# TensorE's order of tile sums and products, and VectorE's order of comparisons, in the relational layers of a seven-layer graph network

## The reference, cut to what matters

```python
m = c[:, 0:1] * (hs @ bases[0])              # hs = h[src], c = coef[etype]
for b in range(1, bases.shape[0]):
    m = m + c[:, b:b + 1] * (hs @ bases[b])
agg = jax.ops.segment_sum(m, dst, num_segments=h.shape[0])
return agg + h @ loopw + bias                # then relu and a residual, three times
...
xt = jnp.einsum('nd,rde->rne', x, W)         # the second relational network, two layers
agg = jax.ops.segment_sum(xt[rel, src], dst, num_segments=x.shape[0])
return jax.nn.relu(agg + x @ SW + b)
```

## Time and profile before

| | |
|---|---|
| median of 3 runs | 7921.8 us (7919.49 to 7972.01) |
| the profiled execution | 7969.38 us, its span 7967.5 us |
| busy: PE, DVE, ACT, POOL | 67%, 42%, 10%, 73% of the span |
| mean granted PE clock | 0.681 of full |

### The profile page before, as it was taken

The page is one execution under the profiler, slowest core; times in us unless marked ns, Lnnn a source line. Parts: engine busy times, 40 slices in busy tenths (PEclk is TensorE's granted clock), DMA queues, the critical chain, the costliest instruction groups (busy, mean ns, idle before and its releaser), DMA issues. The chain is left out here.

```text
span 7967.5 us, 103222 instructions
## 1 busy us (share of the span) xinstructions
PE 5324.7 (67%) x25966; PEld 4686.8 (59%) x25967; DVE 3378.4 (42%) x9384; ACT 821.6 (10%) x1790; POOL 5813.4 (73%) x6265
## 2 busy tenths in 40 slices
PE   6777777777776666677677776666666676644444
PEld 5666656666655555566666675565655566533333
DVE  5444554444455565644444672222222322312222
ACT  1111111111111111100000001111111111100000
POOL 6777767777767777677777427777767777677776
PEclk8777777777766777655555787777777777755555
DMA  3222222222211211222222552222222222212222
GB/s 108 75 74 74 75 69 72 75 74 75 74 49 51 52 52 52 54 63 63 63 63 62 152 173 52 55 56 55 55 53 53 55 55 55 55 52 56 55 55 54
DMA packets 324367, 531.03 MB, mean 67 GB/s; under 512 B 116072, under 2 KB 179733, under 8 KB 323925
## 3 DMA queue, kind: packets, MB, share of 16 engines
q0 software_dynamic: 186496, 383.17, 17.9%
q1 hardware_dynamic: 89185, 119.37, 5.3%
q10 hardware_dynamic: 48500, 26.51, 1.1%
HBM read 448.44 MB, written 80.14 MB: 66 GB/s over the span
## 5 line engine op out<-in xcount | busy, mean ns | idle before, releaser
L608 POOL DMA_INDIRECT ring<-h_table,edges_i x3328 | 3267.7, 982 | 1095.1 <-issue 1078.2
L877 PE MATMUL sum<-onehot,ring 128*128 128x128 f32 x8320 | 1763.1, 343 | 1120.4 <-DMA ring<-h_table,edges_i 901.5
L877 PEld LDWEIGHTS sum<-onehot,ring 128*128 128x128 f32 x8320 | 1373.9, 233 | 1465.5 <-DMA ring<-h_table,edges_i 1015.8
L1176 DVE TENSOR_TENSOR acc<-msg,acc 128x16 f32 x4160 | 728.0, 175 | 2747.3 <-PE msg L884 2214.9
L884 PE MATMUL msg<-work,mix_w 128*128 128x128 f32 x4992 | 1087.2, 406 | 273.5 <-ACT work L687 270.0
L884 PEld LDWEIGHTS msg<-work,mix_w 128*128 128x128 f32 x4992 | 1010.5, 309 | 348.6 <-issue 341.9
L559 POOL DMA_INDIRECT sorted_rows<-ring,pos_i x832 | 850.8, 1023 | 281.5 <-issue 249.3
L687 ACT ACTIVATE work<-sum 128x512 f32<-128x512 f32 x1040 | 621.3, 597 | 3890.4 <-PE sum L877 3823.5
L608 POOL DMA_INDIRECT ring<-in_x_dram,edges_i x832 | 821.1, 987 | 274.5 <-issue 266.5
L591 POOL DMA_INDIRECT ring<-h_table,pos_i x832 | 794.7, 955 | 274.8 <-issue 274.8
L884 PE MATMUL msg<-work,rel_w 128*128 128x128 f32 x3328 | 739.8, 412 | 183.9 <-ACT work L687 183.0
(11 more groups left out here) (198 smaller groups left out, 3483.7 us busy)
## 6 DMA issues: line engine op xcount, KB each, us to landing
ring<-sorted_rows SPq DMA_DIRECT2D x208, 260.0 KB, 3.0
ring<-h_table,edges_i POOLq DMA_INDIRECT x3328, 2.5
edges_i<-bucket_flat SPq DMA_DIRECT2D x208, 208.0 KB
h_table<-rows ACTq DMA_DIRECT2D x78, 256.0 KB
ring<-in_x_dram,edges_i POOLq DMA_INDIRECT x832, 2.5
ring<-h_table SPq DMA_DIRECT2D x832, 8.0 KB
sorted_rows<-ring,pos_i POOLq DMA_INDIRECT x832, 2.3
ring<-h_table,pos_i POOLq DMA_INDIRECT x832, 2.5
```

The lines of the kernel that those rows point to most:

```text
L608: nc.gpsimd.indirect_dma_start(out=rows_in[:, s, :], out_offset=None, in_=rows_of[:, :], in_offset=bass.IndirectOffsetOnAxis(ap=srcT_i[:, ...
L877: last = nc.tensor.matmul(SUM[q % 2][:, t * KEYS:(t + 1) * KEYS], rows_in[:, 4 * q + t, :], onehot[:, 4 * q + t, :], start=True, stop=True)
L1176: nc.vector.tensor_tensor(acc[:, at], MSG[h][:, s * WIN:(s + 1) * WIN], acc[:, at], ALU.add).then_inc(added, 1)
```

## The change

On PE the function `messages` is taken apart into `tile_sums(h, i, k)` (the sums of a half) and `mix(h, k)` (its products). Before, a turn was sums 0, products 0, sums 1, products 1. Now the sums of half 0 of a layer's first turn stand in `opened`, ahead of the loop, and a turn is sums 1, products 0, sums 0 of the next turn (not in the last turn, by a condition on PE), products 1. On DVE both halves' comparisons of the next turn stand between the additions of half 0 and of half 1; before, those of half 1 were made at the front of their own turn, ahead of `rank` or `settle`. In the layers without a norm the number of chunks written out ahead of the loop goes from 4 to 2.

```diff
+SHORT_LAG = 2
...
-    for c in range(LAG):
+    for c in range(lag):
         step(c, c % 2, c // 2, rounds(c))
-    with eng.Fori(LAG // 2, CHUNKS // 2) as n:
+    with eng.Fori(lag // 2, CHUNKS // 2) as n:
...
                     def opened(p):
                         pe.wait_ge(pass_opened, P * r + p + 1)
                         apart(pe)
+                        tile_sums(0, 0, pe.snap(count(P, p, r, 0)))
...
+                    def tile_sums(h, i, k):
+                        for q in (2 * h, 2 * h + 1):
+                            pe.wait_ge(onehot_ready[q], k + 1)
+                            pe.wait_ge(evacuated[(q + 2) % 4], k + 1)
+                            for t in range(4):
+                                pe.wait_ge(gathered[4 * q + t], i * 16 + (GATHER_PASS * r + 16))
+                                last = nc.tensor.matmul(SUM[q % 2][:, t * KEYS:(t + 1) * KEYS], rows_in[:, 4 * q + t, :],
+                                                        onehot[:, 4 * q + t, :], start=True, stop=True)
+                            last.then_inc(summed[q], 1)
+
+                    def mix(h, k):
+                        for q in (2 * h, 2 * h + 1):
+                            pe.wait_ge(evacuated[q], k + 1 + h)
+                        pe.wait_ge(added, k * RING + HALF * h + HALF)
+                        for n in range(N_RELS):
+                            last = nc.tensor.matmul(MSG[h][:, 0:HALF * WIN], W[:, n, :],
+                                                    sums[:, h, n, :, :].rearrange("p t v -> p (t v)"),
+                                                    start=(n == 0), stop=(n == N_RELS - 1))
+                        last.then_inc(messaged[h], 1)
+
                     def messages(i, k):
...
+                        tile_sums(1, i, k)
+                        mix(0, k)
+                        with pe.If(i < TURNS - 1):
+                            tile_sums(0, nc.s_assert_within(i + 1, min_val=1, max_val=TURNS - 1,
+                                                            skip_runtime_bounds_check_because="the condition above"),
+                                      pe.snap(k + 1))
+                        mix(1, k)
...
-                        onehots(0, 0, dve.snap(count(P, p, r, 0)))
+                        first = dve.snap(count(P, p, r, 0))
+                        onehots(0, 0, first)
+                        onehots(1, 0, first)
                         dve.wait_ge(acc_set, 2 + CHUNKS * (r + 1))
 
                     def turn(i, k):
-                        onehots(1, i, k)
                         adds(0, i, k)
                         with dve.If(i < TURNS - 1):
-                            onehots(0, nc.s_assert_within(i + 1, min_val=1, max_val=TURNS - 1,
-                                                          skip_runtime_bounds_check_because="the condition above"), k + 1)
+                            following = nc.s_assert_within(i + 1, min_val=1, max_val=TURNS - 1,
+                                                           skip_runtime_bounds_check_because="the condition above")
+                            for h in range(2):
+                                onehots(h, following, k + 1)
                         adds(1, i, k)
...
                     def turn_ranking(i, k):
-                        onehots(1, i, k)
                         rank(i)
-                        adds(0, i, k)
...
+                        turn(i, k)
```

More of the change, by code:

```diff
@@ L114, in edge_passes, with edge_chunks @@
                 moved(p)
-def edge_chunks(nc, eng, P, more, before, turn, round_end, step, last):
+def edge_chunks(nc, eng, P, more, before, turn, round_end, step, last, lag):
     def rounds(c):
@@ L730, in _ @@
                     edge_passes(act, P, more, r, evacuate)
-                    edge_chunks(nc, act, P, more, r, evacuate_ranking if r < 2 else evacuate, round_end, rows_out, CHUNKS + 2)
+                    edge_chunks(nc, act, P, more, r, evacuate_ranking if r < 2 else evacuate, round_end, rows_out, CHUNKS + 2, SHORT_LAG)
                     continue
@@ L748, in _ @@
                     edge_passes(act, P, more, r, evacuate)
-                    edge_chunks(nc, act, P, more, r, evacuate, round_end, norm_step, CHUNKS + 3)
+                    edge_chunks(nc, act, P, more, r, evacuate, round_end, norm_step, CHUNKS + 3, LAG)
                 else:
@@ L868, in messages_ranking @@
                         sum_pos(i)
-                    def messages(i, k):
[L871 to L887, removed]
@@ L1003, in _ @@
                     edge_chunks(nc, pe, P, more, r, messages_ranking if r < 2 else messages, round_end, rel_step,
-                                CHUNKS + 3 if layer["norm"] else CHUNKS + 1)
+                                CHUNKS + 3 if layer["norm"] else CHUNKS + 1, LAG if layer["norm"] else SHORT_LAG)
                 else:
@@ L1512, in turn_ranking @@
                     def turn_ranking(i, k):
-                        onehots(1, i, k)
                         rank(i)
-                        adds(0, i, k)
-                        with dve.If(i < TURNS - 1):
-                            onehots(0, nc.s_assert_within(i + 1, min_val=1, max_val=TURNS - 1,
-                                                          skip_runtime_bounds_check_because="the condition above"), k + 1)
-                        adds(1, i, k)
+                        turn(i, k)
                     def turn_settling(i, k):
-                        onehots(1, i, k)
                         settle(i)
-                        adds(0, i, k)
-                        with dve.If(i < TURNS - 1):
-                            onehots(0, nc.s_assert_within(i + 1, min_val=1, max_val=TURNS - 1,
-                                                          skip_runtime_bounds_check_because="the condition above"), k + 1)
-                        adds(1, i, k)
+                        turn(i, k)
                     edge_passes(dve, P, more, r, turn, opened, moved)
@@ L1536, in _ @@
                     edge_chunks(nc, dve, P, more, r, turn_ranking if r < 2 else turn_settling if r == 2 else turn, round_end,
-                                rel_step, CHUNKS + 2 if layer["norm"] else CHUNKS + 1)
+                                rel_step, CHUNKS + 2 if layer["norm"] else CHUNKS + 1, LAG if layer["norm"] else SHORT_LAG)
                 else:
```

## The result

| kernel | median, us | runs |
|---|---|---|
| before | 7927.15 (7919.49 to 7972.01) | 8 |
| changed | 7954.38 (7944.55 to 7958.67) | 8 |

The ratio is 1.0034 with a 95% interval of 1.0021 to 1.0048: a loss of 27 us where +6 was forecast. It lies within 1%, and 7954 lies in the range of 7886 to 7990.

What follows compares the result with a forecast made beforehand. POOL's gather issue, 1.26 us each, was taken to bound the relational layers. Layer ends +7.8 and starts -2, all else 0, gave +6 on 7921.8, so 7928 us, range 7886 to 7990.

Steps and rivals of the forecast that it cites:

- POOL's rate is the bound: In the relational layers POOL issues a gather each 1.26 us without a break, and the other engines keep up.
- the saving on PE: Inside a layer, PE's 468 us of idle time before products, waiting for ACT's copy, is hidden; worth 0 us.
- Its own signs of being wrong: POOL waiting for PE inside a layer, the two undisturbed layers leaving 1048 us, or the layer ends not growing.
- It fits with 5 us to spare: First two layers: the new order's loop takes 15.5 us against POOL's 20.8 us a turn; 0 us taken.
- The ring: One turn's loop: sums 0, products 1, `sum_pos`, sums 1, products 0, additions, comparison, sums 0; 15.5 us, 21.7 at lower clock.
- The ends, +7.8: At the five layer ends both products stand behind the last sums: +7.8 us in all, bounds -1 and 14.5.
- The starts, -2: At the first two layers' starts PE's first sums stand ahead of two register loads: 1 us saved each.
- Stretching by DVE, 0, between -35 and +45: First three layers: DVE instructions lengthen POOL's gathers; moving `rank` and `settle` keeps the mean over phases, 0 us.
- The ring becomes the bound: Rival, chance 0.05: PE at 1.2 GHz in the ranking layers makes a turn 21.7 us, not 20.8; some 8020 us.
- Earlier buffers: Rival, chance 0.04: buffers that come free earlier let POOL start earlier, removing its waits for PE; 7920 us.
- the change doesn't do what it says: Rival, chance 0.03: products still wait 0.9 us for ACT's copy, hidden behind gathers except at the ends; 7932 us.
- The condition on PE: The last-turn test on PE in each turn: under 0.1 us a turn, hidden beside POOL's rate, 0 us.

Runs made afterwards that it cites:

- settle_early: Changed kernel with `settle` of the next turn between DVE's comparisons and the additions of half 1, turn 0's ahead of the loop: 7945.84 us, ratio 1.0023.

## Why the prediction was right in its class, and where its sum was off

**POOL's rate is the bound, and the saving on PE is worth nothing.** Right. Products no longer wait for ACT (454 us of idle time in the later profile of before, for the first network's and the second's 271 and 183, now 0), and the two undisturbed layers moved by -0.6 and -1.4 us.

**Its own signs of being wrong.** Two of three came true: POOL waits for PE inside the third layer, and four of the five ends didn't grow by more than 0.8 us. (The third, the undisturbed layers leaving 1048 us, is no sign here: both kernels' later profiles have 1041 to 1043.) The +23 us between the two spans are +26.2 of waits, for which 0 was taken, +10.4 at one end, for which +1.2 was taken, +24.0 of stretching in the first two layers and -32.6 in the third; all else is -5. That 7954 lies in the range is therefore in part luck: the room had been made for stretching, and large parts cancel.

**"It fits with 5 us to spare ... which takes up what a chunk's end adds. I take 0 us."** This step failed. The ring was summed without what stands in DVE's queue between the two groups of additions at a chunk's end in the third layer: the chunk's normalization (4.3 us) and `settle` (6.9 us, with 0.9 behind it). It measured 25.5 us, and +26.2 us of waits. "settle_early" takes the waits away, which shows that `settle` in this place is the cause. The ring also lacked the copy by ACT between `sum_pos` and the sums of half 1, some 2 us a turn in the first two layers; POOL's 20.9 us a turn still covered it.

**The ends, +7.8.** They measured +10.9, the sizes in the wrong places. Four ends moved by -0.8, +0.7, 0.0 and +0.5, where 1.25, 1.25, 1.2 and 2.9 were taken: the clock had come up before the two products, so the pair takes 3.7 to 3.9 us instead of 7.56. The third end moved by +10.4 where +1.2 was taken, for the same `settle` in the same queue.

**The starts, -2.** POOL's waits there changed by +1.1 in all. The first wait did get shorter in the first layer, and was given back by the next.

**Stretching by DVE, 0, between -35 and +45.** It measured +11.4, +12.6 and -32.6, so -9, within the bounds. For the third layer the mechanism was right (the PSUM operand removes it); that the mean over phases stays the same was not, in any of the three layers. I put each gather that lasts over 0.05 us too long to the DVE instruction that ended nearest to 0.84 us before the gather's end. In the first layer L1209 and L1216, the comparison and the scan of `rank`, go from 19.0 us in 92 gathers to 31.7 in 102 with their new line numbers, in the second from 17.3 to 31.8; the growth is the scan's (13.8 to 28.9, and 11.2 to 28.0). No run changed these two, so for them the cause is argued from times alone. In the third L1234 goes from 51.5 in 85 to 20.6 in 50. Why the phases fall as they do wasn't tried. Part of the third layer's relief is bound to its waits: when they were removed, 21 us came back.

**The rivals.** "The ring becomes the bound" was priced by the clock alone. It is what happens at nine chunk ends, and in the third to fifth layer with TensorE's order alone, both times by what stands on DVE inside the ring. It happens in the slower condition too, where the ring grew by steps that come late for a reason that stays open. "Earlier buffers" and "the change doesn't do what it says" did not occur. The condition on PE shows no cost, as the undisturbed layers didn't grow. The 41 us that the figures of the Trainium skill (Advanced Engine Details and Errata, Control Flow Timing) gave for it, if nothing hid it, are not there.

## What to carry to other kernels

When a change puts work of the next step ahead of work of this one, write down the ring for the worst step, not the mean one, with everything that stands in each engine's queue inside it: chunk ends, last turns and side work such as `settle`. Where two edits are made together, ask which of the two makes a ring that the other breaks; timed alone, each tells little of the pair. And if an engine's rate is the bound, look first at what lengthens its own instructions: one operand moved to PSUM was worth more than the reordering of two engines.

## What the runs showed of the hardware that wasn't expected

- **The slower condition.** The same kernel took 7928 to 7932 us in some experiments and 9331 to 9364 in others, on one and the same chip too. POOL's unstretched gather is the same in both (0.95 to 0.96 us). But POOL waits some 200 us a layer in the kernel before. In its fourth layer 99 of the 101 waits over 0.4 us stand before the first gather of a half, where POOL waits for PE's sums. The profile puts 0.8 ms of them to something that it calls "remote". The page gives no time to landing for the gathers, where it gives 2.5 us otherwise. The expectations above speak of packets that start only with the next issue. The DMA view doesn't bear that out: at a layer's start the first packets stand 1.6 us behind the issue in both conditions (5804.1 after 5802.55, and 6848.75 after 6847.11). What is late there stays open. One of the kernel before's 16 executions beside "settle_early" took 11862 us, at a granted clock of 1.0. It isn't in the ratio, has no profile, and stays unexplained.
- **An operand decides.** The product of two SBUF tiles, 128x832, lasts 1.02 us, and a gather that starts 0.05 us into it 1.81. With one operand in PSUM it lasts 1.02 us too, and the gather beside it 0.95.
- **The gather's own duration drifts** between executions of one kernel: the 832 gathers of the fourth layer were busy 795.82 us in the earlier trace rows and 788.28 in the later profile. Over six such stages that is 45 us, more than the effect in question, so two profiles are compared layer by layer only after such an undisturbed layer has been looked at.
